# A gated attention and mixture-of-experts kernel: the add of the masked scores to the base, moved from GpSimd to VectorE

## The reference

```python
def _xattn(h, adj_raw, Wq, Wk, gamma_raw):        # h: (4, 512, 128), adj_raw = layernorm(x): (4, 512, 512)
    sim = einsum(Q, K over all heads) / (sqrt(d) * H)          # (4, 512, 512)
    threshold = top_k(sim, int(512 * 0.3))[0][:, :, -1:]
    A = sigmoid(sim) * (sim >= threshold)
    A = (A + swapaxes(A, -1, -2)) * 0.5
    return (1 - gamma) * adj_raw + gamma * A

x = x + tanh(g_xattn) * _xattn(ctx_512, layernorm(x), ...)
x = x + tanh(g_ffn) * _ffn(layernorm(x), ...)      # a shared expert for every token, and the best 2 of 8 experts
```

## Time and profile before

| | |
|---|---|
| median of 3 runs | 589.0 us (588.94 to 589.23) |
| the profiled execution, its own time | 588.87 us |
| its span, from the first to the last instruction | 587.1 us |
| mean granted TensorE clock, of 2.4 GHz | 0.934 |
| TensorE busy | 494.9 us (84%), 3105 matmuls |
| VectorE busy | 343.4 us (58%), 708 instructions |
| ScalarE busy | 263.1 us (45%), 473 instructions |
| GpSimd busy | 231.5 us (39%), 226 instructions |

### The profile page before, as it was taken

How to read it: one execution, slowest core, us unless ns; L and a number is a source line. 1 busy time by engine, 2 the same in 40 slices (tenths; PEclk the granted TensorE clock), 3 DMA queues, 4 the chain that set the end, 5 groups by cost and what they waited for, 6 DMA issues and landing times.

```text
span 587.1 us, 10965 instructions
## 1 busy us (share of the span) xinstructions
PE 494.9 (84%) x3105; PEld 275.4 (47%) x3106; DVE 343.4 (58%) x708; ACT 263.1 (45%) x473; POOL 231.5 (39%) x226
## 2 busy tenths in 40 slices
PE   2402588879996999778998899999999999999992
PEld 0100343334442444334464566666666666666661
DVE  0589758787868796977993577433333333333331
ACT  1696578736784569524141265322223223222221
POOL 2147835463344524470133034433443443443422
PEclk9855769989998999896999999999999999999998
DMA  3236293204720482025005589454454355345333
GB/s 117 95 85 181 79 303 118 58 18 172 263 57 19 143 291 58 20 73 185 1 0 157 189 222 258 89 91 89 73 88 91 71 82 96 72 78 98 73 40 49
DMA packets 32048, 63.73 MB, mean 109 GB/s; under 512 B 4048, under 2 KB 4304, under 8 KB 32016
## 3 DMA queue, kind: packets, MB, share of 16 engines
q1 hardware_dynamic: 23280, 42.89, 22.5%
q0 software_dynamic: 8736, 20.45, 19.3%
HBM read 41.05 MB, written 22.28 MB: 108 GB/s over the span
## 4 chain that ended last, share of the span: by engine, by line
PE 56%; DVE 18%; ACT 9%; issue 7%; DMA 5%; POOL 2%; SPq 1%; DVEq 1%; POOLq 0%; ACTq 0%
PE py L1021 13%; PE pg L1001 12%; PE pu L1002 12%; PE pg L860 4%; PE pu L860 4%; PE pt_bank L818 4%; DVE w L1195 3%; DVE pa L1154 3%; DVE w L1125 2%; PE pa L1011 2%; ACT w L627 2%; ACT w L633 2%; PE pu L880 1%; DVE w L1158 1%; DVE w L1202 1%
## 5 line engine op out<-in xcount | busy, mean ns | idle before, releaser
L1001 PE MATMUL pg<-w,x_t 128*128 x468 | 140.7, 313 | 0.0
L1002 PE MATMUL pu<-w,x_t 128*128 x468 | 140.7, 313 | 0.0
L555 POOL DMA_INDIRECT out<-rows,idx x39 | 61.8, 1584 | 141.5 <-ACT rows L758 131.4
L1021 PE MATMUL py<-w,work 128*128 x351 | 82.1, 379 | 0.8 <-DVE work L1453 0.8
L860 PE MATMUL pg<-w 128*128 128x512 f16 x288 | 78.2, 388 | 2.4 <-DVE work L1249 2.4
L748 ACT ACTIVATE work<-pg 128x352 f32<-128x352 f32 x39 | 18.1, 464 | 132.1 <-PE pu L1002 132.1
L860 PE MATMUL pu<-w 128*128 128x512 f16 x240 | 66.7, 388 | 0.0
L594 ACT ACTIVATE w<-stage 128x544 f16<-128x544 f32 (+1 forms) x80 | 50.8, 648 | 34.3 <-DMA stage<-in_weights 33.8
L496 POOL TENSOR_TENSOR w<-stage,w 128x544 f16<-128x544 f32 (+1 forms) x43 | 53.5, 1254 | 27.2 <-ACT stage L598 25.3
L1442 DVE SCALAR_TENSOR_TENSOR work<-pu,work 128x352 f32<-128x352 f32 x39 | 20.5, 525 | 62.6 <-ACT work L748 62.5
L1001 PEld LDWEIGHTS pg<-w,x_t 128*128 128x128 f16 x468 | 45.8, 98 | 20.5 <-issue 0.6
(11 more groups left out here) (199 smaller groups left out, 800.4 us busy)
## 6 DMA issues: line engine op xcount, KB each, us to landing
stage<-in_weights SPq DMA_DIRECT2D x80, 272.0 KB, 3.6
w<-in_x SPq DMA_DIRECT2D x4, 1024.0 KB, 6.8
out<-w SPq DMA_DIRECT2D x16, 256.0 KB, 2.8
xn_rows<-w SPq DMA_DIRECT2D x16, 256.0 KB, 4.9
out<-rows SPq DMA_DIRECT2D x13, 256.0 KB, 3.2
rows<-out SPq DMA_DIRECT2D x12, 256.0 KB, 3.3
w<-in_ctx_t SPq DMA_DIRECT2D x4, 256.0 KB, 3.5
out<-rows,idx POOLq DMA_INDIRECT x39, 4.8
```

The source lines that it names most:

```text
L555: pool.indirect_dma_start(out=out, out_offset=bass.IndirectOffsetOnAxis(ap=idx[:, t:t + 1], axis=0), in_=rows[:, t % 2, :], in_offset=None ...
L1001: pe.matmul(pg[p][:, 0:H], lhs, w[:, item, half, at:at + H], start=begin, stop=end)
L1002: mm = pe.matmul(pu[p][:, 0:H], lhs, w[:, item, half, at + H:at + 2 * H], start=begin, stop=end)
L1021: mm = pe.matmul(py[:, :], hid_t[:, p, part * JC + j, :], w[:, item, half, at:at + C], start=(j, part, half) == (0, 0, 0), stop=(j, part) ...
```

## The change

`add_attention` of GpSimd goes, and the same four adds stand in VectorE's `attended`, behind the masks and ahead of everything else of that function. They wait for the base (`base_sb`) and the masked scores (`a_made`) and count on `xa_made` as before. Where GpSimd made the adds of batch 0 it now waits until they are done. In the loop it has no such wait.

```diff
-            def add_attention(b):
-                for i in range(TPB):
-                    after(pool, base_sb, b * TPB + i + 1)
-                    after(pool, a_made, b * TPB + i + 1)
-                    pool.tensor_tensor(xb[:, i, :], xb[:, i, :], att[:, i, :], ALU.add).then_inc(xa_made, 1)
-
...
             first_pieces(0, FIRST)
-            add_attention(0)
+            after(pool, xa_made, TPB)
             first_pieces(FIRST, FIRST + 3)
...
                     if u < TPB:
                         low_piece(b + BEFORE, u)
-                add_attention(b + 1)
                 for n in range(TPB, CHUNKS - 2):
                     low_piece(b + BEFORE, n)
                 row_scalars(b + 1)
...
                     after(dve, x1_made, b * TPB + i + 1)
                     o.mark(dve.bn_stats(bn6[:, 2, i, :], xb[:, i, :]))
 
+                for i in range(TPB):
+                    after(dve, base_sb, b * TPB + i + 1)
+                    after(dve, a_made, b * TPB + i + 1)
+                    dve.tensor_tensor(xb[:, i, :], xb[:, i, :], att[:, i, :], ALU.add).then_inc(xa_made, 1)
                 if shared is not None:
                     shared_rows(shared, 0)
                 for i in range(TPB):
```

## The result

The changed kernel takes 598.11 us (median of 4 runs, 597.11 to 600.10), the kernel before 589.12 us (4 runs) beside it: a ratio of 1.0147, 95% interval 1.012 to 1.0175. It is slower by 9 us. The forecast case had 594.6 us; what came is the rival "the longer idle of TensorE costs it its clock", 596.3 to 598.0, with the median 0.1 us above its upper end.

What follows compares the result with a forecast made beforehand. VectorE's chain was taken to set the end of the four per-batch stretches where scores are masked and added. -0.6 us in batch 0 plus 3 x 2.1 gave +5.7 us, so 588.87 became 594.6 us; range 591.5 to 598.0.

Steps and rivals of the forecast that it cites:

- The forecast case: Whole kernel: the likeliest outcome, +5.7 us on 588.87 us, giving 594.6 us, about 1 us either way; chance 0.55.
- the longer idle of TensorE costs it its clock: Rival: longer idle before TensorE's transposes, batches 1 and 2, brings half clock, 1.7 us a stretch: 596.3 to 598.0; chance 0.24.
- (a): Batches 1 to 3: GpSimd's four adds leave, their collision with masks three and four goes, 2.0 us off the masks.
- (b): Batches 1 to 3: two GpSimd weight pieces move up onto the masks; the 2.0 us come back, masks end as before.
- the freed time is kept: Rival: GpSimd's two pieces miss the masks of batches 1 to 3, so only batch 0 counts: 588.3 us; chance 0.07.
- (c): Batches 1 to 3: VectorE's own four adds run alone and take 2.4 us, at 0.60 each; upper bound 2.8.
- (d): Batches 1 to 3: with L1260's step of 0.65 us, L1209 starts at 131.2 instead of 129.13 in batch 1: +2.1 us.
- (e): Behind VectorE's adds: TensorE has nothing of its own that ends later, so the delay reaches its transposes in full.
- Batch 0, -0.6 us: First batch: GpSimd already waits for the adds, no piece moves up, L1209 comes at 62.4 instead of 63.04: -0.6 us.
- slack took part of the delay: Rival: some wait further on, a load or ScalarE's queue, covers a microsecond per batch: 591.6 us; chance 0.11.
- The two engines take turns: VectorE's masks and GpSimd's SBUF operations exclude each other: a mask costs 0.67 us alone, 1.68 beside a GpSimd operation.

Runs made afterwards that it cites:

- Experiment 1: The changed kernel, but in the loop GpSimd waits for VectorE's four adds before weight pieces 4 and 5: 590.96 us, ratio 1.0017 to the kernel before.
- experiment 2: The changed kernel without VectorE's four adds, GpSimd's pieces staying on masks three and four: 588.97 us, ratio 0.9978 to the kernel before.
- experiments 3 and 4: Changed kernel with GpSimd held until the masks are done: 590.25 us; then also adds as scalar_tensor_tensor, constant factor: 589.41 us, per-row factor: 598.19 us.

## Why the prediction was right, and where it was not

The direction and the mechanism held, step by step:

- (a) and (b), the freed time is taken by the two pieces: as forecast. Their predicted issue was 123.7 to 124.4, in a trace that runs 0.3 us later it was 124.57; the masks took 5.0 us up to the next instruction, before 5.1. Experiment 1 showed that without this nothing is lost. The rival "the freed time is kept", which put L1209 at 129.2 against 129.13, is just that experiment: 0.08 us per batch and a time equal to that of before.
- (c), four adds at 0.60: 2.48 us as a group, steps of 0.60. Nothing near the upper bound.
- (d), +2.1 us per batch: 2.0 in all three. The step of 0.65 us for L1260 doesn't follow from the two rows given for it (128.17 to 129.13 less 0.22 is 0.74), but it was right: 0.66 in the trace after (130.76 to 131.42).
- (e), nothing hides it: right. The idle time of TensorE rose from 0.72 to 2.80 us, as forecast, and experiment 2 brought it to 0.84. From L1206 to the transposes it is 11.0 us in batch 1 before and after, so no slack took part of the delay.
- Batch 0, -0.6 us: -0.7 in the traces. In this profile the half clock at the start took as much back.

Of the 9.0 us measured the forecast had 5.6, and the median of 598.11 lies 0.1 us above the range; by the ratio, on the 589.0 us that the forecast started from, it is 597.7. The step that failed is the choice of the likeliest case: "Forecast (594.6, about 1 us either way): 0.55" against "Half clock (596.3 to 598.0): 0.24". The half clock came in two batches of one profile and in one of two of the other, at the price that I gave it (1.7 us; measured 1.5 to 1.7). I had the row that spoke for it, an idle of 2.66 us in batch 3 with a half-clock stretch behind it, and set against it only that dense work stands on both sides, which no row showed to matter. The half-clock stretch ahead of the expert part I did not see coming, but it belongs to neither kernel: TensorE idles 2.3 to 2.9 us there in all twelve profiles (2.33 before, 2.73 after), and five of them have the stretch. VectorE's stretches give 589.1 + 6.0 - 0.7 = 594.4 us, with one or two half-clock stretches of 1.6 us 596.0 or 597.6. What remains to 598.1 I can't place; the runs of this kernel differ among themselves by 3 us.

The explanation behind step (b) was too simple. "The two engines take turns" is true of the masks and of GpSimd's operations, but experiments 3 and 4 show that it depends on the masks' per-row operand. The Trainium skill (SBUF — State Buffer, Who interferes with whom) calls the pair of ports that VectorE and GpSimd share an exclusive lock. The traces agree: two pieces take 3.31 us beside masks and 2.40 beside L1207. That GpSimd can be kept out for a whole row of VectorE instructions is what experiments 3 and 4 show, and no more is known here of why. It did not matter for the number, because what GpSimd moved onto was the masks.

## What to carry to other kernels

When work leaves an engine, look at what stands behind it in that engine's order, and when that could start: it moves up, onto whatever runs there, and one wait may be worth more than the move (here it gave back 1.3% of the time, all that the move had cost). An added operation of 2.4 us on the engine that sets the end is paid in full unless something on the same chain became shorter. And an idle time of TensorE that grows from 0.7 to 2.8 us may cost another 1.5 to 1.7 us of half clock. Here it did so in three of four cases, and such a case should have got the larger chance.

## What I had not expected of the hardware

Four VectorE additions with both inputs in SBUF take 2.48 us beside GpSimd's pieces when their factor is absent or a constant in the instruction, and 4.65 us when it is read per row from SBUF, with the same data in the same place (experiments 3 and 4). In the first two cases GpSimd, issued in the middle of the row, waited for its end (4.06 us for two pieces that take 2.40 alone). The per-row operand also adds 0.06 to 0.07 us to each step. I did not try which gap it is that lets GpSimd in: the operand itself, or the longer step that comes with it.
